# First attention of an AdaLN block: softmax weights made a second time by key, row maxima carried in spare rows of q

## The chip, the cores and the metric

The kernel runs on one core of a Trainium2 chip. The metric is the device time of one execution in microseconds (us). A core has five engines with a queue each: TensorE (PE), which multiplies, VectorE (DVE), ScalarE (ACT), GpSimd (POOL), and SyncE (SP), which here only starts DMAs. Each engine takes its instructions in order; semaphores connect them.

## The reference

Eight batches of 512 tokens of width 128 pass through a modulated attention with 16 heads of 8 dimensions, then six layers of windowed attention and a feed-forward part. The change touches the first attention alone (and one number in the loop of the rest):

```python
# L0_attn_x: (8, 512, 128); heads = 16, dh = 8
h = _layernorm(x) * (1 + ca) + sa
q = h @ Wq.T
k, v = jnp.split(h @ Wkv.T, 2, axis=-1)
q = q * dh ** (-0.5)
sim = einsum('bhid,bhjd->bhij', q, k)
sim = where(causal_mask, -finfo.max, sim)
e = exp(sim - max(sim, axis=-1))
num = einsum('bhij,bhjd->bhid', e, v)
out = num / (sum(e, axis=-1) + 1e-8)
x = x + ga * (out.reshape(B, N, D) @ Wo.T)
h = _layernorm(x) * (1 + cb) + sb
x = x + gb * ffn(h)            # six layers, the "stack"
```

## The kernel before

`adaln_block` runs three parts one after the other: `modulated_attention` (names with at_ in the trace), `local_stack` (st_) and `last_residual` (lr_). A whole batch's scores do not fit, so the first part goes batch by batch and head by head: `loop` runs `batch(b)` for b = -1 to 8, the middle six (1 to 6) as a hardware loop, the others written out. A `batch` has 16 steps (`AH`), one for each head. Work that belongs to another batch is placed in the steps by an offset: the list `M_JOBS` says at which step, and in which part of it, PE makes which of the products that are needed once for a batch or for a group of four heads. They all go through one PSUM bank, `ps_m`, and each waits until the previous one was taken.

A step treats four blocks of 128 queries (`TILES`), i = 0 to 3, with causal rows of 128, 256, 384 and 512 keys. What one head goes through:

- DVE `pick_head` (L1337) multiplies the group's `q4` by a column that keeps one head's rows, into `qm`. Four heads share the 128 rows, and each number stands as a high and a low part, so that one fast fp32r product gives the score.
- PE `score` (L1056) makes block i into its own bank of four. It waits until ACT has finished the same block of the head before.
- DVE `mask` (L1343) adds the causal block on the diagonal, and `maximum` (L1347) takes the negated row maximum.
- ACT `exponentials` (L1191) writes the weights to `probs` and their row sums to `den`.
- DVE `reciprocals` (L1355, L1357) and POOL (L1426) divide the weights, four multiplies a head.
- PE `transpose` (L1069) turns ten 128x128 blocks three steps later, ACT `copy_transposed` (L1201) moves them to `probT`.
- After four heads PE makes the product with v (job "round", L1095), which DVE copies to `aT` (L1314). After four groups comes "wo" (L1110).

Norms: a mean and a variance by PE, logarithm and exponential by ACT, then a chain of five operations with a Newton step on DVE in `finish_norm` (L1264 to L1284), at the end of steps 12 (the next batch's input norm) and 14 (the last batch's output norm). POOL besides splits the stack's weights in high and low parts (`split`, L1408, L1410, three times a batch) and makes tables.

## Time and profile before

| | us |
|---|---|
| median of 3 runs | 4414.46 (4410.03 to 4418.47) |
| profiled execution, own time | 4412.12 |
| its span | 4410.3 |
| first attention, first to last score | 37.8 to 844 |
| its end, last store to xT | 877.6 |
| PE busy over the whole span | 3768.9 |
| DVE busy over the whole span | 3571.7 |

The page cuts the span into 40 slices of 110 us, so the first eight slices are the first attention. A row of a timeline has the start, the duration, the engine, the line, the operation and its operands, and in brackets how long the engine had been idle and what ended that. Records of PE overlap, so a matmul's duration holds a fixed latency; what a series costs is seen from start to start. The granted clock of PE (PEclk) is 1 at 2.4 GHz and 0.5 at 1.2 GHz.

### The profile page before, as it was taken

The numbers are of one execution on the slowest core, as the hardware profiler recorded it, in microseconds if no ns is written. First come the engines' busy times: TensorE is split into PE (matmuls) and PEld (weight loads), VectorE is DVE, ScalarE is ACT, GpSimd is POOL, SyncE is SP. The second block draws the span as 40 slices with busy tenths as digits, with TensorE's granted clock in tenths as the row PEclk, the third lists the DMA queues.
The fourth block names the chain that finished last, engine by engine and source line by source line (L and its number), as shares of the span: only waits on it lengthen the run. The fifth ranks groups of instructions, "written<-read, shape, count | busy, mean of one in ns | idle before, by whom it ended". The sixth has DMA issues, their size and how long they took to land. (4 is left out here: it accounts for less than half of the span.)

```text
span 4410.3 us, 109941 instructions
## 1 busy us (share of the span) xinstructions
PE 3768.9 (85%) x41516; PEld 2856.2 (65%) x41516; DVE 3571.7 (81%) x5298; ACT 2656.4 (60%) x4035; POOL 2895.4 (66%) x2520
## 2 busy tenths in 40 slices
PE   5666666669999899998999989999899999899996
PEld 3444444357777777776777767777677777677774
DVE  6777777678888788887888878888888888888884
ACT  5666666546666566656566656656566656566663
POOL 3555555357777677676767666777677676667672
PEclk9888888889999999999999999999999999999998
DMA  1111111032222322223222232222322222222221
GB/s 38 53 53 53 53 53 45 8 90 64 55 60 56 92 59 62 56 58 91 62 55 62 56 88 65 55 58 54 89 60 67 56 56 78 70 60 63 56 55 58
DMA packets 157205, 267.21 MB, mean 61 GB/s; under 512 B 32062, under 2 KB 51644, under 8 KB 152380
## 3 DMA queue, kind: packets, MB, share of 16 engines
q1 hardware_dynamic: 157116, 266.19, 22.1%
q8 instruction: 36, 0.59, 0.1%
q14 instruction: 53, 0.43, 0.0%
HBM read 44.81 MB, written 26.21 MB: 16 GB/s over the span
## 5 line engine op out<-in xcount | busy, mean ns | idle before, releaser
L789 POOL TENSOR_TENSOR st_qk_rot<-st_qk_rot,st_qk_sq 128x1024 f32<-128x1024 f32 x384 | 920.4, 2397 | 939.6 <-DVE st_qk_sq L686 939.6
L429 PE MATMUL st_ps<-st_wqkv,st_xs 128*128 128x512 f32 x3456 | 956.7, 412 | 66.2 <-DMA st_wqkv<-wqkv_parts 37.7
L537 ACT ACTIVATE st_qk_sq<-st_ps 128x1024 f32<-128x1024 f32 x384 | 393.9, 1026 | 652.6 <-PE st_ps L429 652.0
L429 PEld LDWEIGHTS st_ps<-st_wqkv,st_xs 128*128 128x128 f32 x3456 | 612.4, 190 | 231.4 <-issue 97.8
L809 POOL TENSOR_TENSOR st_qk_rot<-st_qk_rot,st_rn 128x1024 f32<-128x1024 f32 x384 | 722.7, 1903 | 15.0
L1426 POOL TENSOR_TENSOR at_probs<-at_probs,at_rden 128x128 f32<-128x128 f32 (+3 forms) x512 | 361.8, 738 | 389.6 <-DVE at_rden L1357 389.6
L668 DVE TENSOR_REDUCE st_nt<-st_qk_sq 128x16 f32<-128x1024 f32 x384 | 465.7, 1213 | 175.5 <-ACT st_qk_sq L537 175.4
L686 DVE TENSOR_TENSOR st_qk_sq<-st_ps,st_rot 128x512 f32<-128x512 f32 x768 | 490.2, 678 | 0.0
L672 DVE TENSOR_TENSOR st_qk_rot<-st_ps,st_rot 128x1024 f32<-128x1024 f32 x384 | 465.9, 1213 | 8.6 <-PE st_ps L444 8.6
L444 PE MATMUL st_ps<-consts_sb,st_qk_rot 128*128 128x128 f32 x3072 | 403.0, 274 | 27.9 <-DVE st_hid L769 16.5
L437 PEld LDWEIGHTS st_ps<-st_oT,st_wo 128*128 128x128 f32 x3072 | 368.8, 192 | 79.4 <-issue 75.8
L1191 ACT ACTIVATE at_probs<-at_score,at_nmx 128x128 f32<-128x128 f32 (+3 forms) x512 | 269.1, 527 | 249.0 <-DVE at_nmx L1347 244.3
L444 PEld LDWEIGHTS st_ps<-consts_sb,st_qk_rot 128*128 128x128 f32 x3072 | 357.1, 141 | 93.7 <-DVE st_hid L769 36.3
L568 ACT ACTIVATE st_k_bd<-st_ps 64x1024 f32<-64x1024 f32 x384 | 389.4, 1014 | 3.7 <-PE st_ps L444 1.4
L437 PE MATMUL st_ps<-st_oT,st_wo 128*128 128x128 f32 x3072 | 379.2, 277 | 1.4 <-ACT st_probT L598 1.2
L457 PE MATMUL st_ps<-st_k_bd,st_qT 128*32 128x128 f32 x12288 | 376.1, 275 | 1.8 <-ACT st_v_tok L582 1.8
L1056 PE MATMUL at_score<-at_k,at_qm 128*128 128x128 f32 (+3 forms) x512 | 239.9, 510 | 159.8 <-ACT at_probs L1191 117.6
L469 PE MATMUL st_ps<-st_v_bd,st_probT 128*32 128x128 f32 x12288 | 375.2, 274 | 0.0
L837 POOL TENSOR_TENSOR st_s<-st_s,st_mx 128x1024 f32<-128x1024 f32 x192 | 365.8, 1905 | 9.9 <-DVE st_mx L711 9.9
L707 DVE TENSOR_TENSOR st_s<-st_ps,consts_sb 128x1024 f32<-128x1024 f32 x192 | 234.5, 1221 | 146.4 <-PE st_ps L457 146.4
L457 PEld LDWEIGHTS st_ps<-st_k_bd,st_qT 128*32 128x32 f32 x12288 | 324.4, 110 | 34.4 <-ACT st_v_tok L582 26.2
L469 PEld LDWEIGHTS st_ps<-st_v_bd,st_probT 128*32 128x32 f32 x12288 | 323.8, 110 | 23.0
(125 smaller groups left out, 6828.4 us busy)
## 6 DMA issues: line engine op xcount, KB each, us to landing
st_v_bd<-st_v_tok SPq DMA_DIRECT2D x1152, 128.0 KB, 2.3
st_v_bd<-st_v_tok SPq DMA_DIRECT2D x672, 64.0 KB, 2.1
wqkv_parts<-at_w_parts SPq DMA_DIRECT2D x18, 1024.0 KB, 4.5
st_wqkv<-wqkv_parts SPq DMA_DIRECT2D x18, 1024.0 KB, 5.7
at_w_raw<-in_wqkv SPq DMA_DIRECT2D x18, 512.0 KB, 4.1
rotary_tables<-at_rot SPq DMA_DIRECT2D x6, 512.0 KB, 2.8
st_rot<-rotary_tables SPq DMA_DIRECT2D x24, 128.0 KB, 2.4
st_wo<-in_wo SPq DMA_DIRECT2D x6, 512.0 KB, 4.2
```

The source lines that it names most:

```text
L429: last = pe.matmul(out[:, c * 512:(c + 1) * 512], xs[:, x_part, t * P:(t + 1) * P], rhs, start=(n == 0), stop=(n == len(PASSES) - 1))
L437: last = pe.matmul(out[:, 0:P], wo[:, c, :], oT[:, c * P:(c + 1) * P], start=(c == 0), stop=(c == IC - 1))
L444: last = pe.transpose(out[:, c * P:(c + 1) * P], src[:, c * P:(c + 1) * P], ident)
L457: last = pe.matmul(out[g * WIN:(g + 1) * WIN, c * P:(c + 1) * P], qT[:, par, c * P + g * WIN:c * P + (g + 1) * WIN], k_bd[:, c, :, key:key ...
L469: last = pe.matmul(out[g * WIN:(g + 1) * WIN, c * P:(c + 1) * P], probT[:, c * P + g * WIN:c * P + (g + 1) * WIN], v_bd[:, par, g, :, c * ...
L537: act.activation(qk_sq[:, cols_of(a)], slot_of("qk"[a], 0, t), ACT.Square).then_inc(squared[a], 1)
L568: last = act.activation(k_bd[rows, :, a, WIN + t1 * P:WIN + (t1 + 1) * P], src[rows, :, :], ACT.Copy)
L668: dve.tensor_reduce(nt[:, 2 + par, heads], qk_sq[:, cols].rearrange("p (h d) -> p h d", d=DH), AX.X, ALU.add).then_inc(ss_sum, 1)
L672: dve.tensor_tensor(qk_rot[:, cols].rearrange("p (h d) -> p h d", d=DH), slot_of("qk"[a], 0, t).rearrange("p (h d) -> p h d", d=DH), rot[: ...
L686: last = dve.tensor_tensor(dst[:, :, g, :], src[:, :, 1 - g, :], sines.unsqueeze(1).to_broadcast([P, HEADS, DH // 2]), ALU.mult)
L789: pool.tensor_tensor(qk_rot[:, cols], qk_rot[:, cols], qk_sq[:, cols], ALU.add).then_inc(rot_done[a], 1)
L809: pool.tensor_tensor(view, view, rn[:, par, heads_of(a)].unsqueeze(2).to_broadcast([P, HEADS, DH]), ALU.mult).then_inc(normed[a], 1)
```

## The change

The weights are no longer transposed. The scores are made twice: once by row, only for the maxima, and once by key, where the exponential goes straight into `probT`.

- Each strip of 32 rows (one head) has rows 0 and 1 spare. k has ones there, and q gets the row maximum (negated, high part and rest) there, so the second product is already shifted. `maximum` collects the maxima of four heads, ACT `max_parts` and DVE `max_rest` split them, PE transposes them (job "mt"), DVE adds them to `q4`.
- The causal mask is a matmul that adds into the same PSUM bank (`mask`, `mask_by_key`), not a DVE operation.
- A head is cut from `q4` by a 0/1 mask of strips: by POOL (`pick`, into `qs`) for the first product, by ACT (`pick_shifted`, into `qt`) for the second, six steps later (`LAG`).
- Both kinds of scores go in three units of one bank each (512, 512 and 256 columns). A unit's first product waits for the maxima, or for the exponential, of the same unit of the head before.
- v has a column of ones, so the product with v also gives the sums. After "round" (now taken by ACT), job "den" brings the sums to rows, DVE makes reciprocals and spreads them, job "rd" transposes them, and DVE multiplies `aT`. The divisions of POOL are gone.
- The Newton step of a norm goes to POOL (`newton_step`, steps 11 and 13); DVE keeps one multiply (`gain`) and the last operation (`finish_norm`, steps 12 and 15).
- The jobs have two banks that take turns, and `M_JOBS` is new. By step, "|" before what PE makes at the step's end: 0 den | mt; 1 q | rd; 2 k; 3 round | x; 4 den | mt; 5 q | rd; 6 k | mean0; 7 round; 8 den | mt; 9 rd, q | v; 10 var0, k | wo; 11 round | mean1; 12 den | mt, var1; 13 q | rd; 14 k; 15 round.
- `fill_block` puts additions to an unused semaphore ahead of the loops: 156 on ACT and 116 on DVE in the first attention, 60 on PE, 22 on ACT and 8 on DVE in the stack. They move where the loop's instructions begin in memory. The setup on DVE also spreads the weights `wqk` into strips.

```diff
+AT_FILL = {"act": 156, "dve": 116}
+ST_FILL = {"pe": 60, "act": 22, "dve": 8}
+def fill_block(eng, filled, n):
+    for _ in range(n):
+        eng.sem_inc(filled, 1)
...
-        def loop(eng, unit):
+        def loop(eng, unit, fill=0):
+            fill_block(eng, filled, fill)
...
+LAG = 6
+ROW_UNITS = (((3, 0),), ((2, 0), (0, 3 * P)), ((1, 0),))
+KEY_UNITS = ((0,), (1, 3), (2,))
+PROBT_BUFS, QS_BUFS = 8, 4
...
+                        pe.wait_ge(max_ready, count(b, 0, AH * UNITS, (h - 1) * UNITS + u))
+                    for n, (i, at) in enumerate(ROW_UNITS[u]):
+                        pe.matmul(ps_s[u][:, at:at + (i + 1) * P], qs[:, h % QS_BUFS, i * P:(i + 1) * P],
+                                  k4[:, g, 0:(i + 1) * P], start=(n == 0), stop=False)
+                def mask(u):
+                    for n, (i, at) in enumerate(ROW_UNITS[u]):
+                        last = pe.matmul(ps_s[u][:, at + i * P:at + (i + 1) * P], ident_r[:, :], causal_r[:, :],
+                                         start=False, stop=(n == len(ROW_UNITS[u]) - 1))
+                    last.then_inc(scores_ready, 1)
+                def scores_by_key(b, d, h, u):
+                    g = h // GROUP
+                    if u == 0:
+                        pe.wait_ge(picked_t, count(b, d, AH, h))
                     if not (isinstance(b, int) and b + d == 0 and h == 0):
+                        pe.wait_ge(exp_ready, count(b, d, AH * UNITS, (h - 1) * UNITS + u))
+                    for n, j in enumerate(KEY_UNITS[u]):
+                        pe.matmul(ps_t[:, KEY_AT[j]:KEY_AT[j] + N - j * P], k4[:, g, j * P:(j + 1) * P],
+                                  qt[:, h % 2, j * P:N], start=(n == 0), stop=False)
...
+                        if i % 2 == at % 2 and alive(b, d0 + over):
                             pe.wait_ge(taken[kind0], count(b, d0 + over, PER[kind0], g0))
...
+                def exponentials(b, d, h, u):
+                    act.wait_ge(t_ready, count(b, d, AH * UNITS, h * UNITS + u))
...
+                    act.activation(probT[:, h % PROBT_BUFS, UNIT_COLS[u]], ps_t[:, UNIT_COLS[u]], ACT.Exp,
+                                   scale=float(AD) ** -0.5).then_inc(exp_ready, 1)
+                def pick_shifted(b, d, h):
+                    g, c = divmod(h, GROUP)
+                    if c == 0:
+                        act.wait_ge(taken["mt"], count(b, d, GROUPS, g))
...
+                    act.activation(qt[:, h % 2, :], q4[:, g, :].bitcast(F32), ACT.Copy, scale=strips[:, c:c + 1]).then_inc(picked_t, 1)
...
+                def maximum(b, h, u):
+                    g, c = divmod(h, GROUP)
+                    dve.wait_ge(scores_ready, count(b, 0, AH * UNITS, h * UNITS + u))
...
+                    for i, at in ROW_UNITS[u]:
+                        last = dve.tensor_reduce(nmx[:, g % 2, i, c:c + 1], ps_s[u][:, at:at + (i + 1) * P],
+                                                 AX.X, ALU.max, negate=True)
+                    last.then_inc(max_ready, 1)
...
+                    pool.tensor_tensor(square, root_, root_, ALU.mult).then_inc(newton[second], 1)
...
+                    pool.wait_ge(gained[second], count(b, d, 1, 0))
+                    pool.tensor_tensor(centred, centred, square, ALU.mult).then_inc(normed[second], 1)
...
+                    pool.tensor_tensor(qs[:, h % QS_BUFS, :], q4[:, g, :].bitcast(F32), strips[:, c:c + 1].to_broadcast([P, N]),
+                                       ALU.mult).then_inc(picked, 1)
```

On PE, a step with "round" inside the hardware loop, before. L1056 are scores, L1069 the transposes of the head three steps back, L1095 the product with v:

```order
L1056 MATMUL at_score<-at_k,at_qm 128x128
L1055 REGISTER_ALU
L1056 MATMUL at_score<-at_k,at_qm 128x256
L1069 MATMUL at_t<-consts_sb,at_probs 128x128 x4
L1095 MATMUL at_m<-at_probT,at_v_pad 32x512 x4
L1095 MATMUL at_m<-at_probT,at_v_pad 32x384 x4
L1095 MATMUL at_m<-at_probT,at_v_pad 32x256 x4
L1095 MATMUL at_m<-at_probT,at_v_pad 32x128 x4
L1055 REGISTER_ALU
L1056 MATMUL at_score<-at_k,at_qm 128x384
L1069 MATMUL at_t<-consts_sb,at_probs 128x128 x6
```

The middle and the end of such a step after the change (the last unit's products, then the end of the loop's body). L1088 are scores by row, L1107 by key, L1094 and L1113 the two kinds of mask:

```order
L1107 MATMUL at_t<-at_qt,at_k 128x128
L1094 MATMUL at_s<-at_causal_r,at_ident_r 128x128 x2
L1113 MATMUL at_t<-at_ident_r,at_causal_r 128x128 x2
L1139 MATMUL at_m<-at_probT,at_v_pad 32x512 x4
L1139 MATMUL at_m<-at_probT,at_v_pad 32x384 x4
L1139 MATMUL at_m<-at_probT,at_v_pad 32x256 x4
L1139 MATMUL at_m<-at_probT,at_v_pad 32x128 x4
L1086 REGISTER_ALU
L1088 MATMUL at_s<-at_k,at_qs 128x256
L1107 MATMUL at_t<-at_qt,at_k 128x256
L1094 MATMUL at_s<-at_causal_r,at_ident_r 128x128
L1113 MATMUL at_t<-at_ident_r,at_causal_r 128x128
```

The ten transposes of a step are gone, four products by key and eight masks have come, and the job stands between the second and the third unit.

On ACT, the last step of the loop's body before. L1191 are exponentials by row, L1201 the copies of transposed weights:

```order
L1191 ACTIVATE at_probs,at_den<-at_score,at_nmx 128x256
L1196 REGISTER_ALU
L1201 ACTIVATE at_probT<-at_t 128x512
L1188 REGISTER_ALU
L1191 ACTIVATE at_probs,at_den<-at_score,at_nmx 128x384
L1201 ACTIVATE at_probT<-at_t 128x768
L1188 REGISTER_ALU
L1191 ACTIVATE at_probs,at_den<-at_score,at_nmx 128x512
L972 REGISTER_ALU
L972 COMPARE_AND_BRANCH
```

The last step of the loop's body after the change. L1270 are the exponentials by key, L1240 takes "round", L1280 is `pick_shifted`:

```order
L1270 ACTIVATE at_probT<-at_t 128x512
L1267 REGISTER_ALU
L1270 ACTIVATE at_probT<-at_t 128x512
L1267 REGISTER_ALU
L1270 ACTIVATE at_probT<-at_t 128x256
L1240 ACTIVATE at_aT<-at_m,consts_sb 128x512
L1280 ACTIVATE at_qt<-at_q,consts_sb 128x512
L1001 REGISTER_ALU
L1001 COMPARE_AND_BRANCH
```

Three exponentials stand where four and two copies stood; the pick of the next head's shifted q is the last thing of a step, behind the third exponential and the job's copy.

On DVE, the end of step 14 before, where `finish_norm` stands between the maxima of two heads:

```order
L1347 TENSOR_REDUCE at_nmx<-at_score 128x1
L1264 TENSOR_TENSOR at_sq<-at_rstd 128x512
L1265 REGISTER_ALU
L1266 TENSOR_TENSOR at_sq<-at_sq,at_var 128x512
L1267 ISA
L1267 SCALAR_TENSOR_TENSOR at_xc<-at_xc,mod_sb,at_rstd 128x512
L1269 REGISTER_ALU
L1270 TENSOR_SCALAR at_sq<-at_sq 128x512
L1271 REGISTER_ALU
L1272 TENSOR_TENSOR at_xc<-at_xc,at_sq 128x512
```

After the change, the end of step 15, where the same norm ends:

```order
L1444 TENSOR_REDUCE at_nmx<-at_s 128x1
L1374 ISA
L1374 TENSOR_SCALAR xT_sb<-at_xc,mod_sb 64x512
L1374 ISA
L1374 TENSOR_SCALAR xT_sb<-at_xc,mod_sb 64x512
L1001 REGISTER_ALU
L1001 COMPARE_AND_BRANCH
```

The five operations of the chain have become two halves of one, behind a wait for POOL.

## Rows read from the trace of the kernel before

**Rows 1.** The page's slices: DVE busy and granted PE clock, in tenths.

```profile
DVE  6777777678888788887888878888888888888884
PEclk9888888889999999999999999999999999999998
```

**Rows 2.** Busy time by stretch: scores of all batches, drain, and batch 0's middle.

```profile
38.00:848.00 810.00, 552.58 (x3050) 347.47 (x3050) 607.85 (x1636) 517.34 (x1410) 457.74 (x590) 0.86 0.12 44
848.00:878.00 30.00, 17.09 (x106) 7.86 (x106) 8.95 (x16) 8.58 (x17) 4.85 (x7) 0.78 0.03 10
...
62.00:102.00 40.00, 28.39 (x194) 18.39 (x194) 32.53 (x94) 31.74 (x87) 20.75 (x30) 1.00 0.00 1
```

**Rows 3.** Timeline: first and last score; `hT` of batches 2 and 7.

```profile
37.77 1.51 PE L1056 MATMUL at_score<-at_k,at_qm 128*128 128x128 f32 x4 [1.56 <-DVE at_k L1301]
...
201.48 0.49 DVE L1284 TENSOR_SCALAR at_hT<-at_xc,mod_sb 128x512 f32<-128x512 f32 x1
...
740.78 0.49 DVE L1284 TENSOR_SCALAR at_hT<-at_xc,mod_sb 128x512 f32<-128x512 f32 x1
...
843.92 0.78 PE L1056 MATMUL at_score<-at_k,at_qm 128*128 128x512 f32 x1
```

**Rows 4.** Who waited for whom, 150 to 750 us: total, times, longest.

```profile
ACT at_probs L1191 <- DVE at_nmx L1347: 192.6, 154, 6.7
PEld at_score L1056 <- ACT at_probs L1191: 150.3, 113, 7.0
```

**Rows 5.** Timeline: `finish_norm` on DVE, PE's next score, and the loop's first DVE operation.

```profile
406.46 1.92 DVE L1264 TENSOR_TENSOR at_sq<-at_rstd 128x512 f32<-128x512 f32 x1
...
408.42 2.71 DVE L1266 TENSOR_TENSOR at_sq<-at_sq,at_var 128x512 f32<-128x512 f32 x1
...
415.06 0.47 PE L1056 MATMUL at_score<-at_k,at_qm 128*128 128x128 f32 x1 [6.68 <-ACT at_probs L1191]
...
434.51 0.49 DVE L1337 TENSOR_SCALAR at_qm<-at_q,consts_sb 128x512 fp32r<-128x512 f32 x1 [2.08 <-issue]
```

**Rows 6.** Groups by line and form, 150 to 750 us: busy, mean ns, idle before.

```profile
L1343 DVE TENSOR_TENSOR at_score<-at_score,consts_sb 128x128 f32<-128x128 f32 x355 | 104.3, 294 | 116.6 <-PE at_score L1056 116.6
L1347 DVE TENSOR_REDUCE at_nmx<-at_score 128x1 f32<-128x512 f32 x88 | 59.9, 681 | 0.0
L1301 DVE SCALAR_TENSOR_TENSOR at_k<-at_high,consts_sb,at_m 128x512 fp32r<-128x512 f32 x22 | 16.3, 739 | 0.0
...
L1191 ACT ACTIVATE at_probs<-at_score,at_nmx 128x256 f32<-128x256 f32 x89 | 41.8, 469 | 81.3 <-DVE at_nmx L1347 81.3
L1163 ACT ACTIVATE at_high<-at_q_full 128x512 fp32r<-128x512 f32 x22 | 13.9, 630 | 0.7
...
L1426 POOL TENSOR_TENSOR at_probs<-at_probs,at_rden 128x512 f32<-128x512 f32 x89 | 97.4, 1095 | 0.0
```

**Rows 7.** Timeline: series on PE, and ACT copies that answer to PE.

```profile
401.10 2.36 PE L1095 MATMUL at_m<-at_probT,at_v_pad 128*32 128x512 f32 x32
...
854.47 1.30 ACT L1201 ACTIVATE at_probT<-at_t 128x768 f32<-128x768 f32 x2 [3.19 <-PE at_t L1069]
...
855.34 1.31 PE L1069 MATMUL at_t<-consts_sb,at_probs 128*128 128x128 f32 x10 [0.46 <-ACT at_probT L1201]
...
857.11 0.88 PE L1069 MATMUL at_t<-consts_sb,at_probs 128*128 128x128 f32 x6 [0.46 <-ACT at_probT L1201]
...
858.02 0.81 ACT L1201 ACTIVATE at_probT<-at_t 128x768 f32<-128x768 f32 x1 [0.48 <-PE at_t L1069]
...
862.74 0.19 PEld L1110 LDWEIGHTS at_m<-at_aT,at_wo 128*128 128x128 f32 x1 [0.24 <-issue]
...
1600.08 1.23 PEld L429 LDWEIGHTS st_ps<-st_wqkv,st_xs 128*128 128x128 f32 x6
```

**Rows 8.** Timeline of POOL: the divisions of two undisturbed steps of the last batch.

```profile
821.78 2.75 POOL L1426 TENSOR_TENSOR at_probs<-at_probs,at_rden 128x128 f32<-128x128 f32 x4 [5.20 <-DVE at_rden L1357]
825.73 2.75 POOL L1426 TENSOR_TENSOR at_probs<-at_probs,at_rden 128x128 f32<-128x128 f32 x4 [1.19 <-DVE at_rden L1357]
```

More of the change, by code:

```diff
@@ L1059, in transpose @@
[L1059 to L1071 removed]
+                pe.wait_ge(rounded, 2)
@@ L1073, in m_product, with mask_by_key @@
+                def mask_by_key(u):
+                    for n, j in enumerate(KEY_UNITS[u]):
+                        last = pe.matmul(ps_t[:, KEY_AT[j]:KEY_AT[j] + P], causal_r[:, :], ident_r[:, :],
+                                         start=False, stop=(n == len(KEY_UNITS[u]) - 1))
+                    last.then_inc(t_ready, 1)
                 def m_product(b, job):
                     kind, d, g = job
-                    back = [m[2:] for m in M_JOBS].index(job)
+                    out = m_bank(kind, g)
+                    back = at = [m[2:] for m in M_JOBS].index(job)
@@ new lines, in batch @@
+                        for u in range(UNITS):
+                            if alive(b, dt):
+                                exponentials(b, dt, ht, u)
+                            if u == 0:
+                                d, h = head_of(s, 1)
+                                if h % GROUP == GROUP - 1 and alive(b, d):
+                                    max_parts(b, d, h // GROUP)
+                            took = {0: jobs_at(s - 1, 1, "v"), 1: jobs_at(s - 1, 0, "var0") + jobs_at(s - 1, 1, "mean0", "mean1", "var1"),
+                                    2: jobs_at(s, 0, "round", "q", "k")}[u]
@@ L1287, in finish_norm @@
-                    dve.sem_inc(x_done if second else h_ready, 1)
+                            last = dve.tensor_scalar(columns_of(b, d, rows, first), xc[rows, 1, :], 0.5,
+                                                     modulation(b, d, SB, rows), ALU.mult, ALU.add)
+                        last.then_inc(x_done, 1)
+                    else:
+                        if alive(b, 0):
+                            dve.wait_ge(ready["k"], count(b, 0, GROUPS, GROUPS - 1))
+                            dve.wait_ge(ready["v"], count(b, 0, 1, 0))
+                        dve.tensor_scalar(hT[:, :], xc[:, 0, :], 0.5, modulation(b, d, SA),
+                                          ALU.mult, ALU.add).then_inc(h_ready, 1)
```

430 lines of the change are left out of this document (230 added, 200 removed), and 11 rows, old and new, of the table M_JOBS.

## The prediction

> **What bounds the kernel now.** I read the slices first [rows 1]: the first attention is the first eight of 40 slices, where DVE is busy for six to eight tenths and PE's clock falls to 0.8, against 0.9 later. The stack is not changed except in where its loops begin, so the question is what 840 us of attention become. By the stretches [rows 2] its 128 heads take 810 us, 6.33 us a head, with DVE busy for 608, PE for 553, ACT for 517 and POOL for 458: nobody is full. The waits say why [rows 4]: ACT waits 193 us of 600 for DVE's maxima, PE 150 us for ACT's exponentials. It is a ring. PE needs the bank, ACT frees it only after DVE has masked it and taken its maximum, and DVE has other work in between.
>
> That other work is dear in two places [rows 5]. A `finish_norm` stands between two heads on DVE; its first two operations took 1.92 and 2.71 us there, since POOL was splitting weights on the same memory, and PE then began its next score after 6.68 us of idleness. And DVE's first operation of a pass of the loop waited 2.08 us for nothing but its own instructions. From batch 2's `hT` at 201.48 to batch 7's at 740.78 [rows 3] are five batches at 107.9 us. The last batch, without splits, has heads at 3.95 us apart where nothing disturbs them [rows 8]; 16 of those would be 63 us.
>
> **The prices.** At full clock, from [rows 7]: an f32 product of 512 columns starts two records 0.43 us apart (0.19 + 0.24), so q, k, a mean or a variance is 0.86 and "wo" 8 x 0.43 = 3.45. An fp32r product of 512 columns is 0.21 (six weight loads in 1.23, (1.23 - 0.19) / 5). A block of 128 with its own weight load is 0.11 (ten in 1.31, six in 0.88). "round" is 2.36 with the latency, 2.15 without. From [rows 6]: ACT takes 0.47 for 256 columns, of which its successor overlaps some 0.1 ([rows 7]: two copies in 1.30, the larger alone 0.81), hence 0.38, and 0.63 for 512 columns from SBUF, 0.60 with the overlap; DVE 0.68 for a maximum over 512 and 0.74 for an operation on two inputs; POOL 1.1 for 512 columns. From the end of PE's series to ACT's copy are 0.03 us (857.11 + 0.88 to 858.02); back from ACT to PE I take 0.2.
>
> **The new masks.** No row has an fp32r product of 128 columns that adds to a bank. The nearest is the transposed block, 0.11. It cannot be under 0.05 (a quarter of the 0.21 for 512 columns) and at worst its weight load of 0.19 lies bare. I take 0.11; eight masks a head are then 0.9 us, with ends of 0.4 and 1.5.
>
> **A step after the change.** DVE loses four masks (0.29 each), the pick, the reciprocals and most of two norms. It keeps four maxima, under 2.7 us (4 x 0.68), and some 1.4 of takes a step (five of 0.74 for four heads, ten for 16), so it is no longer the ring. ACT loses four accumulator reads and the copies. POOL has 1.1 for the pick, and in a batch six operations of 1024 columns at 2.2 for the splits and eight at 1.1 for the Newton steps, 1.4 a step: no bound either. What is in line now is this: the shifted q of the next head is the last thing in ACT's step; it stands behind the third exponential, which needs PE's last unit, and PE's next product by key needs that q. From one first product by key to the next, at full clock:
>
> - units one and two on PE: 0.21 and two masks 0.22; then 384, 128, 384, 128 columns at 0.54 and four masks 0.44: 1.41
> - the step's job, m
> - unit three on PE: 0.22 + 0.22, latency 0.16, to ACT 0.03: 0.63
> - ACT: exponential 0.38, the take of q, k or "round" 0.60 if there is one, pick 0.60; back to PE 0.2: 1.18 or 1.78
>
> That is 3.23 a step, 51.7 for 16. Jobs in the middle: 4 "den" at 0.88 (eight weight loads at 0.11), 8 q or k at 0.86, 4 "round" at 2.15, one "rd" 0.46, one variance 0.86: 20.3. Twelve takes by ACT: 7.2. Bank waits: where a job's bank was last read by DVE's take of q or k at the start of the same step (steps 2, 6, 7, 10, 11, 14), DVE is done 1.9 after the start (first unit ready at 0.5, 0.68, 0.74) and PE is there at 1.4: 6 x 0.5 = 3.0. Step 13 adds 0.4 for its bank and 0.55 where ACT's logarithm and exponential (2 x 0.63) push the third exponential: 0.95. At the steps' ends: v waits for DVE and adds 0.35; "wo" starts 1.2 us after the unit, because its bank waits for the variance's take, runs 3.45, and is covered by 1.97: with the next score 2.9; the second variance waits for the spread of the reciprocals, 1.3. Together 4.6. Sum: 51.7 + 20.3 + 7.2 + 3.0 + 0.95 + 4.6 = 87.7 us a batch.
>
> The masks' ends make it 80 or 98 (16 steps x 8 x -0.06 or +0.08). For what disturbs it I add 4: the clock will not be full all the time, and splits will still meet DVE's spreads. So 92 us against 107.9 in the loop, and I keep 88 to 100.
>
> **From a batch to the total.** Six batches cost B each. Batch 7 lacks the next one's norm, 0.95 B. Batch 0 has no products by key in six steps and no "wo": some 68 of 92, 0.75 B. So the scores take 7.7 B = 708 instead of 810: -102. Ahead of them: the weights' spread and two more fills, about 3.4 on DVE; 116 fills on DVE between the modulation and x, where I have no duration in these rows and take 3 (ends 1 and 7); the Newton step by POOL, 4 x (1.1 - 0.74), +1.5; less one ACT copy, -0.6. That is +7. ACT's 156 fills lie beside DVE's setup. In the drain, before 30 us [rows 2]: six steps of products by key instead of three, at 1.0 on PE and 1.4 on ACT each, +7; den and rd with their takes between the last "round" and "wo", +3; the norm by POOL, +1.5: +11. The stack stays: in it I found no wait of PE that comes at the head of a pass and not elsewhere. Total -102 + 18 = -84. The profiled execution took 4412.1, 2.3 under the median of the runs shown; against the median that is **4330**.
>
> In general T = 4414.5 - 810 + 18 + 7.7 B = 3622 + 7.7 B, and the change stops paying at B = 103.
>
> **The rivals.**
>
> *The clock is lost (slower).* All prices of PE above are for 2.4 GHz. In the chain 57 us of a batch are PE's (32 of the units, 20 of jobs, 4 to 5 of "wo" and variance), and at 1.2 GHz they double. With a share s of them at the low level B = 88 + 57 s + 3; 103 is passed at s = 0.21. Before, the mean was 0.86 [rows 2], which is a share of 0.28, and by that B is 107 and the time 4446. For it: after the change PE waits in every step, 1.2 to 1.8 us for ACT. Against it: in batch 0 the clock was 1.00 for 40 us with PE busy for 28 of them [rows 2], at steps of 5 us with like gaps, and the long idleness of 6.68 us [rows 5] is what goes. The Trainium skill has a rule on that side (TensorE: Matmul & The Clock Gate, "A second HAM failure mode: psum-queue depth-cycling"): a PE that idles briefly and often while it cycles through PSUM banks can keep switching its clock. By that rule the turn of each step would suffice; the 40 us of batch 0 speak against it. Chance 0.10.
>
> *POOL takes DVE's place.* DVE's `finish_norm` waits for POOL, and the next head's maxima stand behind it. POOL's queue from step 13 on is a pick 1.1, a Newton step 4.4, a pick, a split of 2 x 2.2, a pick: 12.1 us in three steps, which take some 17. By the sum above it is done in time. If both norms and three splits come 2 us late, B = 92 + 8 = 100 and the time is 4392. Chance 0.13.
>
> *The turn is hidden better.* If DVE's and ACT's takes are early enough that bank waits and the tails of steps cost nothing, B = 88 - 8.5 + 2 = 81 and the time is 4246; the masks at 0.05 give the like. Chance 0.10.
>
> *The fill does not do what it says.* If DVE still waits 2.1 us in each pass, +13: 4343, inside the range. If in the stack a loop now begins worse, PE would wait up to 2.1 in 45 passes, +95: 4425. The Trainium skill (Runtime: NRT & Kernel Launch, "Instruction fetch mechanics") has engines read ahead in blocks of 256 instructions and wait where a branch goes back outside the two that are held; by it a body that begins at a border and is under 256 long, as on DVE and ACT now, loses the wait. The rows show the wait alone, not its cause. Chance of the bad case 0.03.
>
> **How the numbers follow.** The forecast has 0.64, the others 0.10, 0.13, 0.10 and 0.03. The range is 4265 (B = 83.5) to 4400 (B = 101): it takes in POOL's case and leaves out the lost clock, the bad fill and half of the better hidden turn. Faster by over 0.2% (9 us, about what a measurement of this kernel tells from no change) holds the forecast, POOL's case and the hidden turn but for their edges: 0.85. Same: 0.05. Slower: 0.10.
>
> **What would show it.** In the changed profile the first attention ends near 795 instead of 878. A batch from `hT` to `hT` is 92. PE's largest wait is for ACT's shifted q, 1.2 to 1.8 in each step; a step with a "round" is about 6 us, one with "den" 4.1. "wo" is followed by a late first product by key. PE's clock in the attention is 0.93 or more. DVE's 2.1 us at the head of a pass are gone, and one pass of the stack is what it was. I am wrong if PE's waits for DVE's maxima lead, if a step without takes is over 4.5 at full clock (then the masks or the way back from ACT are mis-sized), or if the clock stays at 0.86.

## The result, and the profile after

The changed kernel took 4336.7 us (median of 4 runs, 4333.2 to 4340.0) where the kernel before took 4413.2 beside it: a ratio of 0.9825, with a 95% interval of 0.9808 to 0.9842. The forecast was 4330 with a range of 4265 to 4400. The profiled execution of after took 4333.2, its span is 4331.4 and its mean granted clock 0.98.

The page of after, the same two lines of its slices as in [rows 1]. The first attention now ends within the eighth slice, and the drop of PE's clock to 0.6 there is the border to the stack:

```profile
DVE  3555555488888888888888878888888888788884
PEclk9999999699999999999999999999999999999998
```

The stretches of after: batch 0, batch 1, the five batches of the loop, batch 7, the drain, the head of the stack, the rest. Columns: length, then the busy time of PE, PEld, DVE, ACT and POOL with their instructions, PE's clock, DMA share, GB/s.

```profile
54.00:110.00 56.00, 44.93 (x241) 33.21 (x241) 32.67 (x72) 22.41 (x43) 17.32 (x17) 0.94 0.05 15
110.00:197.60 87.60, 70.94 (x489) 51.51 (x489) 47.17 (x101) 44.96 (x86) 32.96 (x32) 1.00 0.13 46
197.60:644.80 447.20, 363.17 (x2460) 261.86 (x2460) 255.21 (x522) 229.66 (x435) 212.29 (x190) 0.99 0.18 65
644.80:743.60 98.80, 79.92 (x566) 58.46 (x566) 55.15 (x115) 50.77 (x96) 30.85 (x26) 1.00 0.04 14
743.60:796.00 52.40, 33.64 (x172) 21.55 (x168) 10.24 (x19) 16.82 (x32) 4.93 (x4) 0.71 0.02 5
```

The loop's clock is 0.99, against 0.86 in [rows 2]. DVE is busy for 57% of the loop, PE for 81%.

One line each: the register step ahead of `hT`, once in each of the loop's six passes, so that (last - first) / 5 is the time of a batch; and the first and last weight load of the scores. Columns: count, durations in ns, first and last start.

```profile
L1382 DVEq FUSED_REGOPS  x6: 53/53/53, 197.2 to 644.3; - x6
L1088 PEld LDWEIGHTS at_s<-at_k,at_qs x512: 186/191/338, 54.2 to 743.6; 128*128 128x128 f32 x171
```

A batch takes (644.3 - 197.2) / 5 = 89.4 us; by [rows 3] it was 107.9. I call this number B. The scores last 689.4 us (before 806.2), which is 7.71 B. They begin 16.4 us later than in [rows 3] (37.77), and from the last one to the end of the attention are 53.2 us (before 33.7). The stack with all that follows it takes 3534.6, before 3532.7. So -116.8 + 16.4 + 19.5 + 1.9 = -79.0, the difference of the two spans.

The largest waits of after between 150 and 700 us (us in total, times, longest), which answer to [rows 4]:

```profile
ACT at_probT L1270 <- PE at_t L1113: 262.6, 285, 3.9
DVE at_nmx L1444 <- PE at_s L1094: 231.8, 194, 4.3
POOL at_qs L1528 <- DVE at_q L1395: 204.4, 19, 12.4
POOL at_sq L1512 <- ACT at_rstd L1263: 84.1, 12, 8.5
PE at_t L1107 <- ACT at_qt L1280: 71.9, 75, 1.5
```

ACT, DVE and POOL wait for PE or for what it made, and PE's own largest wait is for the shifted q (`at_qt`). The last line counts PE's products alone, 0.96 us each in 75 of the some 98 steps of this window. DVE, the former centre of the ring, is behind PE. One step of the loop, with the key projection as its job, in order of time (start, duration, idle time before it in brackets):

```profile
473.54 0.50 PE L1107 MATMUL at_t<-at_qt,at_k 128*128 128x512 f32 x1 [1.06 <-ACT at_qt L1280]
...
475.54 1.12 PE L1161 MATMUL at_m<-at_hT,at_wqk 128*128 128x512 f32 x2 [0.31 <-DVE at_q L1395]
...
476.80 0.27 PE L1113 MATMUL at_t<-at_ident_r,at_causal_r 128*128 128x128 f32 x1
...
477.11 0.38 ACT L1270 ACTIVATE at_probT<-at_t 128x256 f32<-128x256 f32 x1 [1.25 <-PE at_t L1113]
477.39 0.68 ACT L1234 ACTIVATE at_high<-at_m,consts_sb 128x512 fp32r<-128x512 f32 x1
477.96 0.72 ACT L1280 ACTIVATE at_qt<-at_q,consts_sb 128x512 fp32r<-128x512 f32 x1
478.73 0.19 PEld L1107 LDWEIGHTS at_t<-at_qt,at_k 128*128 128x128 f32 x1 [1.69 <-ACT at_qt L1280]
478.74 0.50 PE L1107 MATMUL at_t<-at_qt,at_k 128*128 128x512 f32 x1 [1.38 <-ACT at_qt L1280]
```

This is the turn: the last mask of unit three, ACT's exponential, its take, its pick, and PE's next product by key, 5.20 us after the one before. PE stood idle for 1.38 of them, waiting for the pick.

The ends of the attention, DVE's queue. The first line follows the 116 fills, the others are the drain:

```profile
32.35 0.69 DVE L1423 COPY at_xr<-at_m 128x512 f32<-128x512 f32 x1 [11.27 <-issue]
...
783.80 0.75 DVE L1419 SCALAR_TENSOR_TENSOR at_x<-at_m,mod_sb,xT_sb 128x512 f32<-128x512 f32 x1 [5.55 <-PE at_m L1170]
...
795.82 0.98 DVE L1374 TENSOR_SCALAR xT_sb<-at_xc,mod_sb 64x512 f32<-64x512 f32 x2 [3.62 <-POOL at_xc L1519]
```

### The profile page after: what moved, and what is told of

Read it like the earlier page. It is cut to its first block and busy times, and to the rows that moved or that the text cites. A ratio compares the mean times of both kernels' runs of the same rounds, so it can differ in the third digit from the quotient of the medians.

```text
span 4331.4 us, 109584 instructions
## 1 busy us (share of the span) xinstructions
PE 3791.1 (88%) x42284; PEld 2925.6 (68%) x42284; DVE 3346.0 (77%) x4472; ACT 2494.9 (58%) x3301; POOL 2742.1 (63%) x2200
## 5 line engine op out<-in xcount | busy, mean ns | idle before, releaser
L1444 DVE TENSOR_REDUCE at_nmx<-at_s 128x1 f32<-128x512 f32 (+3 forms) x512 | 238.1, 487 | 296.4 <-PE at_s L1094 295.6
L1270 ACT ACTIVATE at_probT<-at_t 128x512 f32<-128x512 f32 (+1 forms) x384 | 201.6, 526 | 333.5 <-PE at_t L1113 333.5
L1528 POOL TENSOR_TENSOR at_qs<-at_q,consts_sb 128x512 fp32r<-128x512 f32 x128 | 132.9, 1055 | 292.4 <-DVE at_q L1395 269.8
```

## The experiments

Each is an edit of the changed kernel. In all of them B is read from the same line as above, and "the stack" is what lies between the end of DVE's last `xT_sb` of the attention and the end of the span (3534.6 us in the changed kernel). A ratio is against the kernel before, run beside it.

**1. Is it the turn? The pick ahead of the third exponential.**

```diff
                         for u in range(UNITS):
+                            if u == UNITS - 1:
+                                d, h = head_of(s, LAG - 1)
+                                if alive(b, d):
+                                    pick_shifted(b, d, h)
                             if alive(b, dt):
                                 exponentials(b, dt, ht, u)
...
-                        d, h = head_of(s, LAG - 1)
-                        if alive(b, d):
-                            pick_shifted(b, d, h)
```

> One part of the changed kernel is moved: ACT makes the shifted q of the next head ahead of its third exponential instead of at the end of the step; no instruction is added or taken away. Theory (the turn of a step bounds the attention: PE's third unit, ACT's exponential, its take, its pick, PE's next product by key): the pick of 0.72 us and the take of 0.6 leave the chain, PE's idle time ahead of the first product by key (57.6 us for 80 heads) nearly goes, and a batch from hT to hT falls from 89.4 to 76 to 84 us: 4337 - 7.7 x 9 = 4265 us (4230 to 4300). Rival (PE is full enough and DVE's maxima are next behind the pick, within 0.2 us): the wait only changes its name, a batch stays over 87 us and the time over 4315.

Measured: 4249.4 us, ratio 0.9625 (0.9603 to 0.9647). Its register line, and its window 200:560, where the changed kernel has PE at 292.60 and a clock of 0.99:

```profile
L1383 DVEq FUSED_REGOPS  x6: 53/53/53, 179.2 to 581.6; - x6
200.00:560.00 360.00, 325.74 (x2225) 249.67 (x2223) 238.56 (x469) 204.71 (x392) 190.52 (x170) 0.95 0.21 75
```

B = 402.4 / 5 = 80.5, and PE's wait for `at_qt` falls from 46.1 us to 1.2 in this window. The theory holds: with no instruction more or less, 87 us go when ACT's last operation leaves the line. PE is now busy for 90% of the time. What it waits for next:

```profile
PE at_m L1146 <- DVE at_mx_cols L1453: 12.5, 13, 1.8
```

**2. The turn made longer: the pick twice as wide.**

```diff
-        qs, qt = sb("qs", [P, QS_BUFS, N], F32R), sb("qt", [P, 2, N], F32R)
+        qs, qt = sb("qs", [P, QS_BUFS, N], F32R), sb("qt", [P, 4, N], F32R)
...
-                                  qt[:, h % 2, j * P:N], start=(n == 0), stop=False)
+                                  qt[:, h % 2 * 2, j * P:N], start=(n == 0), stop=False)
...
-                    act.activation(qt[:, h % 2, :], q4[:, g, :].bitcast(F32), ACT.Copy, scale=strips[:, c:c + 1]).then_inc(picked_t, 1)
+                    act.activation(qt[:, h % 2 * 2:h % 2 * 2 + 2, :], q4[:, g:g + 1, :].bitcast(F32).to_broadcast([P, 2, N]), ACT.Copy, scale=strips[:, c:c + 1]).then_inc(picked_t, 1)
```

> ACT writes each shifted q twice, into two places beside each other, in one instruction of 1024 columns instead of 512; the products read the first. Instruction counts stay. By the widths of ACT's exponentials (598 against 384 ns) this is 0.43 us more on ACT at the end of each step and nothing else. Theory of the turn: all of it is paid, 16 x 0.43 = 6.9 us a batch, B = 96 and the time 4337 + 53 = 4390. Rival (PE, or the ring of DVE's maxima, bounds the steps): ACT has 43 of 89 us of a batch idle, so under 2 us a batch and under 4352.

Measured: 4468.5 us, ratio 1.0120 (1.0093 to 1.0147). Its pick, its register line and its window:

```profile
L1280 ACT ACTIVATE at_qt<-at_q,consts_sb 128x1024 fp32r<-128x1024 f32 x55 | 63.0, 1145 | 0.0
L1382 DVEq FUSED_REGOPS  x6: 53/53/53, 217.2 to 742.7; - x6
200.00:560.00 360.00, 290.86 (x1691) 207.99 (x1690) 173.79 (x357) 180.91 (x299) 149.40 (x134) 0.87 0.16 55
```

The pick takes 1.145 us instead of 0.719, which is 16 x 0.43 = 6.8 us a batch as expected. But B = 105.1, which is 15.7 more. Neither theory had that. PE waits for `at_qt` for 54.1 us in this window, in 44 cases, and the clock is 0.87: this is the first rival of the prediction, the lost clock, brought about by 0.43 us in each step. Whether it explains the other 8.9 us the next run tells.

**3. The wide pick with more work for PE in its wait.**

```diff
                     def scores(b, h, u):
...
+                    for _ in range(3 if u == 0 else 0):
+                        pe.matmul(ps_s[0][:, :], qs[:, h % QS_BUFS, 3 * P:4 * P], k4[:, g, :], start=True, stop=True)
                     for n, (i, at) in enumerate(ROW_UNITS[u]):
```

PE's fills at the head of the stack are 28 instead of 60 here, since the added products move its loop there too; the stack takes 3533.9 us, as in the changed kernel (3534.6).

> The shifted q written twice in one instruction (as in the run pick_wide), and ahead of each head's scores PE makes three more fp32r products of 512 columns into the bank of the first unit, which the scores then overwrite. They take 3 x 0.21 us and stand where PE waits 1.2 to 1.9 us for ACT's shifted q, so nothing else gets later at an equal clock. Theory (pick_wide fell to a clock of 0.86 because PE did too little per step; its own cost is the 6.9 us): the clock comes back to 0.97 or more, a batch takes 96 to 97 and the time is 4390 to 4400. Rival (the short waits themselves, one or two in each step, make the clock fall, whatever PE does between them; or something else costs the other 9 us): the clock stays under 0.9 and the time is 4460 to 4480.

Measured: 4406.4 us, ratio 0.9982 (0.9971 to 0.9994).

```profile
L1384 DVEq FUSED_REGOPS  x6: 53/53/53, 212.5 to 703.9; - x6
200.00:560.00 360.00, 312.55 (x1998) 228.78 (x1996) 185.19 (x385) 193.75 (x321) 158.73 (x142) 0.97 0.17 60
```

With 48 more products a batch, B falls from 105.1 to 98.3 and the clock rises from 0.87 to 0.97. So 6.8 us of the wide pick's price came back with the clock, 6.8 were the pick's, and some 2 us are left that I didn't take apart (the expectation had 96 to 97). PE still waits for `at_qt` in this kernel, 38 times in the window against 44 in the last one, for 30.2 us against 54.1, through the same banks. A short wait in most steps does not by itself take the clock away: the changed kernel has 48 of them in the window, 46.1 us, at 0.99. The rule of the Trainium skill that the prediction set beside this rival (TensorE: Matmul & The Clock Gate, "A second HAM failure mode: psum-queue depth-cycling"), that a PE idling briefly and often while it cycles through PSUM banks can keep switching its clock, is not borne out where PE has work around its waits.

**4. The price of the masks.** The kernel computes an attention without the causal mask inside the diagonal blocks.

```diff
                             if alive(b, dt):
                                 scores_by_key(b, dt, ht, u)
-                            if alive(b, 0):
-                                mask(u)
-                            if alive(b, dt):
-                                mask_by_key(u)
...
-ST_FILL = {"pe": 60, "act": 22, "dve": 8}
+ST_FILL = {"pe": 188, "act": 22, "dve": 8}
```

> The mask products, eight blocks a head, are left out, so that the kernel computes an attention without the causal mask inside the diagonal blocks; PE gets 128 more fills ahead of the stack, so that its loop there begins where it did. By the prediction's sum a mask is 0.11 us on PE's path, so 16 x 8 x 0.11 = 14 us a batch: B = 75, the time 4337 - 108 = 4229. If a mask costs 0.05 it is 6.4 a batch, 4288. Rival (masks run beside a wait for ACT's exponentials or DVE's maxima): under 3 us a batch, over 4314.

Measured: 4497.3 us, ratio 1.0189 (1.0161 to 1.0216), 268 us over what was expected. Its register line, and a wait in its stack (1000 to 4000 us) that the changed kernel doesn't have among its largest:

```profile
L1380 DVEq FUSED_REGOPS  x6: 53/53/53, 178.2 to 559.5; - x6
PE st_ps L457 <- issue: 168.7, 39, 4.7
```

In the attention it did as the sum says: B = 76.3, 13.1 us less for 128 masks a batch, 0.102 us each. The loss is in the stack: 3794.2 us, 259.6 more than before the edit, though no operation of the stack was touched. The place of PE's loop in the stack is not what it was: a mask leaves two rows in the trace, a weight load and a product, and the expectation counted one, so that the 128 extra fills did not undo the shift but made one (worked out, not shown: no run leaves the masks out with 60 fills). The Trainium skill ("Runtime: NRT & Kernel Launch", "Instruction fetch mechanics") has blocks of 256 instructions; by that the 384 masks of the program at two each are three whole blocks and asked for no fill beyond the 60. What such a shift costs was so far unknown, and runs 6 and 7 are about it.

**5. The fills ahead of the attention.**

```diff
-AT_FILL = {"act": 156, "dve": 116}
-ST_FILL = {"pe": 60, "act": 22, "dve": 8}
+AT_FILL = {}
+ST_FILL = {"pe": 60, "act": 178, "dve": 124}
```

> The fills ahead of the attention (156 on ACT, 116 on DVE) are moved to the head of the stack, so that only the attention's loops begin elsewhere. Theory: the start is 11.3 us earlier (DVE's idle time over its fills), and if the loops' place matters, DVE's wait of about 2 us returns in each of six passes at a place where a finish or the maxima stand behind it: at most 13. Sum within 4325 to 4340, and at the border 0 to 12 more where the fills now stand. Rival (the place of the loops carries the gain of this change): a batch rises from 89.4 to over 93.

Measured: 4330.9 us, ratio 0.9808 (0.9785 to 0.9830), where the changed kernel has 0.9825 (0.9808 to 0.9842): no difference that I can claim. Its register line, and its first and last batch:

```profile
L1382 DVEq FUSED_REGOPS  x6: 53/53/53, 192.0 to 639.2; - x6
42.70:102.70 60.00, 50.44 (x241) 39.71 (x241) 33.01 (x70) 22.32 (x43) 17.52 (x17) 0.82 0.04 14
639.60:745.10 105.50, 87.41 (x566) 65.38 (x566) 55.28 (x115) 50.73 (x96) 30.83 (x26) 0.92 0.03 13
```

B = 89.4, the same to a tenth. The first score starts 11.4 us earlier, and some 13 us are lost in batches 0, 1 and 7, where the clock was 0.82, 0.97 and 0.92 instead of 0.94, 1.00 and 1.00, with the same instructions. But this is the profiled execution, 4338.6 us and the slowest of the four; the others took 4329.1 to 4331.3, so that this loss is that execution's, and the median shows little of it. DVE has no wait of the kind "issue" in its loop, without the fills as with them. So the 2.1 us at the head of a pass in [rows 5] did not go because the loop begins at a border. Its body fell from 355 to 196 instructions by the rest of the change; that this is the reason is argued, not shown.

**6. The fills ahead of the stack.**

```diff
-ST_FILL = {"pe": 60, "act": 22, "dve": 8}
+ST_FILL = {}
```

> The fills at the head of the stack (60 on PE, 22 on ACT, 8 on DVE) are left out, so that the stack's three loops begin elsewhere. A run above had the loop of PE in the stack begin 128 further and lost 246 us there by waits of PE for nothing but its own instructions. Theory (the fill of the stack is what keeps PE's loop where it was in the kernel before, and is worth its place): PE waits in each of 45 passes, 2 to 5 us a pass, 4337 + 90 to 240 = 4425 to 4575. Rival (60 are too few to matter): 4337 less 2 to 6 us of fills, 4331 to 4337.

Measured: 4539.0 us, ratio 1.0294 (1.0262 to 1.0327). The wait that is new in its stack (1000 to 4000 us):

```profile
PE st_ps L457 <- issue: 131.6, 39, 4.6
```

B = 89.4 again; the stack takes 3729.0 us, 194.4 more. In 3000 us of it PE waits 39 times, 3.4 us each, for nothing but its own instructions, at the projections that open a pass. Its waits of this kind at another line (L505) are shorter, 50.2 us for 94.4, and the clock in this stretch is 0.97 instead of 0.99 (0.96 in experiment 4), so that the loss is not the bare wait alone and is not split here. Over 45 passes the stack's loss is 4.3 us a pass, with PE's loop 60 off; in experiment 4, with 128 off, it is 5.8.

**7. Which of these fills?**

```diff
-ST_FILL = {"pe": 60, "act": 22, "dve": 8}
+ST_FILL = {"pe": 60}
```

> At the head of the stack only PE keeps its 60 fills; ACT's 22 and DVE's 8 are left out. The run without all three lost 202 us, with waits of PE up to 4.6 us for nothing but its own instructions in each pass. Theory (it is PE's place alone): the time is 4331 to 4340 and PE's waits of that kind ahead of the stack's first projection are gone. Rival (ACT's and DVE's loops, of 111 and 132 instructions, lose something too when they begin 22 and 8 earlier): up to 2.1 us in 45 passes, over 4350.

Measured: 4341.9 us, ratio 0.9833 (0.9812 to 0.9853), 2 us over the theory's range and not to be told from the changed kernel. The stack takes 3538.2, and PE's waits in it begin with another line, the one that the changed kernel has too:

```profile
PE st_ps L505 <- issue: 100.3, 162, 1.6
```

It is PE's place alone. The stack is "unchanged" in the result only because 60 empty instructions hold PE's loop where it stands well.

**8. The Newton steps back on DVE.**

```diff
                 def finish_norm(b, d, second):
 
+                    dve.tensor_tensor(square, root_, root_, ALU.mult).then_inc(newton[second], 1)
...
+                    dve.tensor_tensor(square, square, variance, ALU.mult).then_inc(newton[second], 1)
...
+                    dve.tensor_scalar(square, square, -1.0, 3.0, ALU.mult, ALU.add).then_inc(newton[second], 1)
...
+                    dve.tensor_tensor(centred, centred, square, ALU.mult).then_inc(normed[second], 1)
                     dve.wait_ge(normed[second], count(b, d, 1, 0))
...
-                        if s == 11 and alive(b, 1):
-                            newton_step(b, 1, False)
-                        if s == 13 and alive(b, -1):
-                            newton_step(b, -1, True)
```

DVE has 81 fills ahead of the attention instead of 116, and POOL 36 ahead of the stack.

> The Newton step of both norms goes back from POOL to DVE, where it stands ahead of the norm's end (three operations on two inputs at 0.74, one at 0.47, four waits for the one before); fills are set so that the stack's loops begin where they did. Theory (the turn bounds, DVE has 38 of 89 us of a batch idle): DVE is 3.1 us later in two steps of a batch, of which 2.4 are its idle time in a step: 1 to 2 us each, B = 91 to 93, less 3 us at start and drain, 4346 to 4362. Rival (DVE's queue between two heads still sets the time, and the move of the norms is what the change lives on): 3.1 us for each norm and a lower clock by the longer waits, B = 96 or more and the time over 4385.

Measured: 4375.1 us, ratio 0.9917 (0.9902 to 0.9932), between the two theories.

```profile
L1392 DVEq FUSED_REGOPS  x6: 53/53/53, 194.9 to 672.8; - x6
200.00:560.00 360.00, 292.40 (x1860) 210.90 (x1858) 202.60 (x422) 173.27 (x329) 128.46 (x119) 0.93 0.18 62
PE at_m L1161 <- DVE at_q L1410: 5.2, 3, 1.7
PE at_m L1146 <- DVE at_mx_cols L1462: 5.5, 8, 1.6
```

B = 95.6, 6.2 more, nearly the rival's 96. The waits that are new are the theory's: 5.2 us, where it was 1.0, for the projection of step 13, whose bank DVE frees late behind the first norm, and 5.5, where it was 2.9, for the row maxima; together 6.8 in 360, or 1.8 us a batch. The rest, about 4.4, goes beside a clock of 0.93 instead of 0.99. So of the 18.5 us a batch that the change brought, 6 hang on where the Newton steps are done.

**9. POOL's slack.** Each pick of POOL is written twice, in one instruction of 1024 columns; `qs` has twice the places, and the products read every second one.

```diff
-                    pool.tensor_tensor(qs[:, h % QS_BUFS, :], q4[:, g, :].bitcast(F32), strips[:, c:c + 1].to_broadcast([P, N]),
+                    pool.tensor_tensor(qs[:, h % QS_BUFS * 2:h % QS_BUFS * 2 + 2, :], q4[:, g:g + 1, :].bitcast(F32).to_broadcast([P, 2, N]),
+                                       strips[:, c:c + 1].unsqueeze(2).to_broadcast([P, 2, N]),
                                        ALU.mult).then_inc(picked, 1)
```

> POOL writes each picked q twice in one instruction of 1024 columns instead of 512, which is 1.0 us more on POOL in each of 128 steps (42 of 89 us of a batch busy, then 59), and 0 more instructions. Theory (POOL is no bound, two heads ahead with its picks, and the Newton steps have time): 0 to 2 us a batch, 4337 to 4352. Rival (POOL takes DVE's place, as the prediction put it: the Newton steps stand behind 3 us more of picks, the norms and the splits come late, and DVE's operations on two inputs wait for POOL's memory): B = 96 to 100 and the time 4385 to 4420.

Measured: 4399.0 us, ratio 0.9967 (0.9955 to 0.9979). POOL is busy for 209.1 of 360 us instead of 169.8, B = 97.9, the clock 0.91. The rival's price came, but not by its way: DVE waits for no Newton step of POOL in this window, and POOL's pick takes 1.91 us instead of 1.06. An operation of DVE by form, first in this kernel, then in the changed one (count, busy us, mean ns, idle us before):

```profile
L1452 DVE TENSOR_TENSOR at_mx_cols<-at_nmx,at_mx_cols 128x16 f32<-128x16 f32 x15 | 13.4, 895 | 0.1
```

```profile
L1452 DVE TENSOR_TENSOR at_mx_cols<-at_nmx,at_mx_cols 128x16 f32<-128x16 f32 x16 | 5.4, 340 | 0.1
```

The rest of the row maxima, 16 columns, takes 895 ns instead of 340. The timeline of the wide pick's run shows why, once with POOL at its pick and once without:

```profile
425.64 1.22 DVE L1452 TENSOR_TENSOR at_mx_cols<-at_nmx,at_mx_cols 128x16 f32<-128x16 f32 x1
...
450.14 0.17 DVE L1452 TENSOR_TENSOR at_mx_cols<-at_nmx,at_mx_cols 128x16 f32<-128x16 f32 x1
```

```profile
424.92 1.90 POOL L1528 TENSOR_TENSOR at_qs<-at_q,consts_sb 128x1024 fp32r<-128x1024 f32 x1
```

POOL's pick ends at 426.82 and DVE's small operation at 426.86, although it began 1.22 earlier; at 450.14, between two picks of POOL, the same operation needs 0.17. The Trainium skill says in "SBUF — State Buffer", "Who interferes with whom", that DVE and GpSimd share a pair of ports under an exclusive lock; the trace agrees. PE waits for what is late:

```profile
PE at_m L1146 <- DVE at_mx_cols L1452: 12.6, 11, 2.2
PE at_m L1186 <- DVE at_rden_rows L1408: 5.5, 4, 1.4
```

In the changed kernel these two are 2.9 and 2.1 us, so 3.6 us a batch more here, and the other 4.9 of the 8.5 go beside the lower clock.

**10 to 12. What is left on the table.** First the early pick without fills ahead of the attention (as in 5), then with PE's 60 fills as the only ones, then also with the row maxima split earlier, by ACT (`max_parts`, first two pieces) and by DVE (`max_rest`, the last piece). The lines below show this last edit alone:

```diff
                     for s in range(AH):
                         dt, ht = head_of(s, LAG)
+                        d, h = head_of(s, 1)
+                        if h % GROUP == GROUP - 1 and alive(b, d):
+                            max_parts(b, d, h // GROUP)
...
-                            if u == 0:
-                                d, h = head_of(s, 1)
-                                if h % GROUP == GROUP - 1 and alive(b, d):
-                                    max_parts(b, d, h // GROUP)
...
-                            if u == 1:
+                            if u == 0:
                                 d, h = head_of(s, 1)
```

> The early pick together with the fills moved away from the head of the attention (156 on ACT, 116 on DVE, now at the head of the stack). Theory (the two effects are apart): 4249 less the 11.4 us by which the first score was earlier, and as in the run without these fills some of it may be lost to the clock of the first and the last batch; 4236 to 4244. Rival (now that the turn is shorter, the place of DVE's or ACT's loop body counts): a batch from pass to pass rises from 80.5 to 82 and more, and the time is 4250 or above.

> The early pick, no fills ahead of the attention, and at the head of the stack PE's 60 alone. Theory (ACT's and DVE's fills bound nothing anywhere): 4236 less what 178 and 124 fills cost at the border, which lie beside PE's drain of the attention only in part: 4225 to 4237. Rival (ACT's and DVE's loops in the stack need their place): over 4250.

> As early_pe_fill, and the splitting of a group's row maxima comes earlier: ACT's copy of the upper parts ahead of the first exponential of its step, DVE's rest behind the step's first maximum instead of its second. In the trace of pick_early PE waited 12.5 us in 360 for these parts (1.8 us at most at one place), 2.8 us a batch. Theory (with the turn shortened these waits are in line): 2 to 2.8 us a batch, 15 to 20 us less than early_pe_fill. Rival (PE is at 0.9 of the time by now and the next wait, for the takes of q, takes its place): under 5 us.

Measured: 4236.5 us, ratio 0.9606 (0.9593 to 0.9619); 4238.3 us, ratio 0.9605 (0.9589 to 0.9622); 4216.8 us, ratio 0.9551 (0.9535 to 0.9567). The register lines of the second and the third, and the wait that the third was made for:

```profile
L1383 DVEq FUSED_REGOPS  x6: 53/53/53, 166.5 to 562.5; - x6
```

```profile
L1382 DVEq FUSED_REGOPS  x6: 53/53/53, 165.1 to 543.0; - x6
PE at_m L1146 <- DVE at_mx_cols L1452: 4.0, 4, 1.0
```

B is 79.1 (by the same line, 167.6 to 563.3), 79.2 and 75.6. Without the fills ahead of the attention the early pick gains 12.9 us (4249.4 to 4236.5), as much as the 11.4 at the start and a little more. The 178 and 124 fills on ACT and DVE at the border cost nothing: the stack's part is 3538.3 with and without them, so that they lie beside other work there, and the expectation of up to 12 us less was too high by that (4238.3 lies 1 us above its range). The earlier split brings 3.6 us a batch, 21 us in all, a little over the 15 to 20 expected; PE's wait at that line went from 12.1 to 4.0 us in the window, which is about 1.8 of the 3.6, and the clock from 0.97 to 1.00. The last kernel is 120 us faster than the changed one, and beats both.

## Why the prediction was right, point by point

**The ring and its place.** Right. DVE left the centre, and PE's largest wait is for ACT's shifted q. But it is smaller than told: 71.9 us in 75 cases, 0.96 each and in three steps of four, where 1.2 to 1.8 in every step was told. Runs 1 and 2 show that this turn sets the time: shortened it gave 87 us; lengthened by 6.8 us a batch it cost 15.7, all of the delay and the lost clock with it.

**The price of a batch.** Told 92, from a sum of 87.7 and 4 for disturbance; measured 89.4. The step with q behind the norm (step 13) took 5.12 (told 5.64), the one with k 5.20 (5.19), with "round" 6.31 (5.98), with "den" 4.20 (4.11). From the end of the last mask to the next product by key I had 1.81 with a take, and the step above has 1.67: ACT's three operations took 1.57 (told 1.58), and the way back to PE is 0.06 and not 0.2. The masks were taken at 0.11 and are 0.102. Of the 4 us for disturbance 1.7 came, as the balance of all this.

**From a batch to the total.** The factor 7.7 is 7.71. The scores came to 689.4 where 708 was told, 19 less, which is 7.7 times the 2.6 that a batch was shorter. The 810 that they were set against was 806.2 by the same measure, so the term itself was 15 off.

**Ahead of the scores.** The term that was mis-sized: 116 fills on DVE were taken at 3 us with ends of 1 and 7, and took 11.27, 0.097 us each, outside the bounds. All else there, told as 4.3, is 16.4 - 11.3 = 5.1. Run 5 has it from the other side: without the fills the first score is 11.4 us earlier.

**The drain.** Told +11, measured +19.5. The step that failed is "six steps of products by key instead of three, at 1.0 on PE and 1.4 on ACT each". The last product by key starts at 770.0, 26.4 us behind the last score, 4.4 us a step, since a step in the drain is still a turn with its jobs and PE's clock is at 0.71 there. Three such steps more are 13 and not 7; with the other terms as told (3 and 1.5) that makes 17.5, and 2 us stay open.

**The clock.** Told 0.93 or more, measured 0.99 in the loop. But the rival's price was wrong. I let PE's 57 us of the chain grow by the share s of 0.28 and came to B = 107; yet 0.28 is a share of time, and in that time only half as much work is done, so that the share of the work is 0.14 / 0.86 = 0.16 and B is 88 + 9 + 3 = 100. Runs 2 and 3 measured the like: at 0.87 a batch lost 6.8 us against 0.97. By the prediction's own formula the clock of before then gives 4392, which is not slower: the condition that the rival named does not carry its chance of 0.10 for slower. A lost clock could still make the kernel slower, as run 2 shows at 0.87 with B = 105.1, but there 6.8 us of it are the pick's. On the other hand the clock was closer to falling than I had thought: 0.43 us in each step sufficed.

**POOL takes DVE's place.** Rightly a rival with its price (B = 100, measured 97.9 in run 9 with POOL's pick doubled), and rightly not the case. The mechanism was mis-told: not the Newton chain comes late, but DVE's small operations meet POOL on the memory and PE waits for those, for 3.6 of the 8.5 us a batch; the rest goes beside the clock of 0.91.

**The turn is hidden better.** Told 81 with a chance of 0.10, not the case; bank waits and tails were paid (row maxima, variance, `aT`: 2.9, 4.0 and 4.0 us in 360). It was to be had by an edit: run 1 has B = 80.5.

**The fill does not do what it says.** Half right. In the attention it did nothing (run 5) and costs 11.3 us at the start. In the stack it does a great deal, 194 us (run 6), all by PE (run 7). The prediction read the fill as something about ACT and DVE, whose bodies are under 256 long, took PE's 60 for nothing, priced a badly placed loop in the stack at up to 2.1 us a pass where 4.3 and 5.8 were measured, and gave 0.03 to the bad case. The total was not hurt by this, since the 60 stand in the change as it is.

**The sum.** -102 + 18 = -84 was told, -116.8 + 16.4 + 19.5 + 1.9 = -79 measured. The closeness is partly luck: the scores were 15 better, the two ends 18 worse.

What stays open: how the 12 us a batch besides the Newton steps split between masks on PE, picks and row maxima (the weights' second making was not undone as a whole); why PE waits where its loop in the stack stands 60 or 128 off; and what share of the losses in runs 8 and 9 is the clock's, which only runs 2 and 3 separate.

## What to carry to other kernels

When a wait between two engines is the largest, look at what the producer does last in its step and whether the consumer needs just that: an operation moved up cost nothing and gave more than the whole change before it (87 us against 77). Where a loop's place in the instruction stream can matter, an edit elsewhere must be followed by a look at every later loop, PE's first, because a few products more or less are paid in another stage. And price a delay on PE above its length while the granted clock has room to fall: in run 2 a delay of 6.8 us a batch cost 15.7.

## What the runs showed of the hardware

- A loop of PE that began 60 instructions off its place lost 4.3 us in each of 45 passes, at 128 off (by the working in experiment 4) 5.8 us, beside a clock of 0.97 and 0.96 instead of 0.99; ACT's and DVE's loops 22 and 8 off, and in the attention 156 and 116 off, lost nothing that can be measured. The Trainium skill ("Runtime: NRT & Kernel Launch", "Instruction fetch mechanics") lets an engine wait where a branch goes back outside what it holds; that fits a wait at the first projection of a pass, but it doesn't tell why the place should matter so much for a body that is much longer than a block (798 products a pass, each with a weight load).
- An empty instruction that only counts up a semaphore took 97 ns on DVE (116 in 11.27 us; in run 8, 81 in 8.02).
- The granted clock fell from 0.99 to 0.87 for 0.43 us more of waiting in a step of 5.6 us, and rose to 0.97 when PE did three more products of 512 columns in that wait.
- A DVE operation on 16 columns took 0.17 us alone and 1.22 beside a pick of POOL, with whose end it ended; in the mean 340 ns, and 895 with POOL's picks doubled.
